# Low parts of the experts' first weights on VectorE in halves in place of GpSimd in quarters, and new places for all steps

## What is computed

```python
def _L0_xattn_ref(q, kv, mem, w_q, w_kv, w_concat):
    c = jnp.concatenate([mem, kv], axis=1)          # mem and kv are the same context
    qh = (q @ w_q).reshape(B, L, 16, 16).transpose(0, 2, 1, 3)
    k, v = split(c @ w_kv)
    attn_prob = softmax(einsum('bhid,bjd->bhij', qh, k) / sqrt(16))
    return (einsum('bhij,bjd->bhid', attn_prob, v)...) @ w_concat

def _L0_ffn_ref(x, ...):
    attn_out = layer_norm(residual, attn_nw, attn_nb)
    combine, dispatch = top1_gate(attn_out, wg, capacity)      # 8 experts, 256 rows each
    dispatched = einsum('sec,sm->ecm', dispatch, attn_out)
    h = gelu(einsum('ecm,emi->eci', dispatched, inter_w) + inter_b)      # 256 -> 1024
    expert_out = einsum('eci,eim->ecm', h, output_w) + output_b          # 1024 -> 256
    moe_out = einsum('sec,ecm->sm', combine, expert_out)
    rh = gelu(attn_out @ res_inter_w + res_inter_b)
    coef = softmax(attn_out @ res_coef)
    return (rh @ res_output_w + res_output_b) * coef[:, :1] + moe_out * coef[:, 1:] + residual

x = x + _L0_xattn_ref(_layernorm(x), ctx, ctx, ...)
x = x + _L0_ffn_ref(_layernorm(x), ...)
```

## Time and profile before

| | |
|---|---|
| median of 3 runs | 384.92 us (384.37 to 385.04) |
| the profiled execution | 384.03 us, span 382.3 us, mean granted clock 0.976 |
| TensorE matmuls | 339.3 us busy, 89% of the span |
| ScalarE | 222.4 us, 58% |
| VectorE | 217.9 us, 57% |
| GpSimd | 199.4 us, 52% |
| w1l on GpSimd | 50.7 us, 32 x 1.595 us |
| w2l on VectorE | 33.6 us, 32 x 1.073 us |
| hl on VectorE | 29.9 us, 32 x 0.945 us |
| DMA | 49.83 MB, mean 130 GB/s |

### The profile page before, as it was taken

The page is one execution under the profiler, slowest core; times in us unless marked ns, Lnnn a source line. Parts: engine busy times, 40 slices in busy tenths (PEclk is TensorE's granted clock), DMA queues, the critical chain, the costliest instruction groups (busy, mean ns, idle before and its releaser), DMA issues.

```text
span 382.3 us, 6412 instructions
## 1 busy us (share of the span) xinstructions
PE 339.3 (89%) x2234; PEld 276.1 (72%) x2234; DVE 217.9 (57%) x533; ACT 222.4 (58%) x429; POOL 199.4 (52%) x251
## 2 busy tenths in 40 slices
PE   3748889999999999999999999899989889889990
PEld 2535447767867867867866766788979889889990
DVE  4346547735625753763754632323589999798640
ACT  3312754863663563563663573629898698788630
POOL 4421421698374458358346424469366675677223
PEclk9966999999999999999999999999999999999997
DMA  6586596413144049046443001018443784795113
GB/s 182 182 238 181 165 294 234 124 56 96 44 123 123 0 138 313 5 146 163 146 135 98 2 16 41 3 56 271 114 154 64 226 259 111 235 260 143 16 15 41
DMA packets 51335, 49.83 MB, mean 130 GB/s; under 512 B 4764, under 2 KB 48488, under 8 KB 51304
## 3 DMA queue, kind: packets, MB, share of 16 engines
q1 hardware_dynamic: 48232, 45.21, 39.2%
q0 software_dynamic: 3072, 4.21, 5.6%
HBM read 33.65 MB, written 15.63 MB: 129 GB/s over the span
## 4 chain that ended last, share of the span: by engine, by line
PE 77%; DVE 6%; ACT 5%; issue 5%; DMA 3%; SPq 1%; POOL 1%; POOLq 0%; ACTq 0%
PE ubank L656 23%; PE mbank L838 15%; PE mbank L656 11%; PE pbank L741 4%; PE mbank L651 4%; PE sbank L709 4%; PE mbank L843 4%; PE mbank L844 3%; PE mbank L845 3%; PE sbank L731 3%; PE pbank L750 2%; DVE smax L1074 2%; ACT h L981 1%; DMA qstack<-dram_q 1%; DMA out_rows<-yrow,rowid 1%
## 5 line engine op out<-in xcount | busy, mean ns | idle before, releaser
L981 ACT ACTIVATE h<-ubank,vecT 128x256 f32<-128x256 f32 x128 | 53.1, 466 | 29.7 <-PE ubank L656 29.5
L838 PE MATMUL mbank<-w2r,h 128*128 128x256 f32 x256 | 62.0, 384 | 2.3 <-ACT h L981 1.0
L656 PE MATMUL ubank<-ao,w1r 128*128 128x256 f32 x256 | 59.7, 382 | 0.0
L612 POOL TENSOR_TENSOR w1l<-w1e,w1h 128x512 fp32r<-128x512 f32 x32 | 50.7, 1595 | 17.0 <-ACT w1h L859 16.8
L838 PEld LDWEIGHTS mbank<-w2r,h 128*128 128x128 f32 x256 | 46.9, 190 | 9.8 <-issue 2.6
L1074 DVE TENSOR_REDUCE smax<-sbank 128x4 f32<-128x512 f32 x64 | 42.0, 686 | 17.5 <-PE sbank L709 16.6
L656 PEld LDWEIGHTS ubank<-ao,w1r 128*128 128x128 f32 x256 | 47.0, 190 | 6.0
L915 ACT ACTIVATE p<-sbank 128x512 f32<-128x512 f32 x64 | 35.8, 596 | 17.4 <-PE sbank L731 17.4
L843 PE MATMUL mbank<-w2h,hh 128*128 128x256 f32 x128 | 36.9, 288 | 9.3 <-issue 7.4
L624 POOL DMA_INDIRECT out_rows<-yrow,rowid x16 | 26.6, 1663 | 29.7 <-DVE yrow L1213 28.5
L844 PE MATMUL mbank<-w2l,hh 128*128 128x256 f32 x128 | 36.0, 281 | 0.0
(11 more groups left out here) (139 smaller groups left out, 700.4 us busy)
## 6 DMA issues: line engine op xcount, KB each, us to landing
w1e<-in_L_ffn_inter_w SPq DMA_DIRECT2D x8, 1024.0 KB, 7.6
w2e<-in_L_ffn_output_w SPq DMA_DIRECT2D x8, 1024.0 KB, 11.0
qstack<-dram_q SPq DMA_DIRECT2D x16, 384.0 KB, 4.3
dram_q<-qpart SPq DMA_DIRECT2D x8, 384.0 KB, 2.7
dispatched<-zrow SPq DMA_DIRECT2D x4, 516.0 KB, 4.8
drow<-dispatched SPq DMA_DIRECT2D x8, 258.0 KB, 2.7
xs<-in_x SPq DMA_DIRECT2D x8, 256.0 KB
ctxs<-in_ctx SPq DMA_DIRECT2D x8, 256.0 KB
```

What stands on the lines that cost most here:

```text
L612: pool.tensor_tensor(quarter(w1l[e % SETS], q), w, quarter(w1h[e % 2], q).bitcast(f32), ALU.subtract).then_inc(sem("w1_low"), 1)
L656: last = nc.tensor.matmul(dst, w[kc], v[kc], start=(kc == 0), stop=(kc == len(w) - 1))
L838: last = nc.tensor.matmul(b[:, 0:D], h[:, n % 2, f, t * P:(t + 1) * P], w2[:, f, :], start=(f == 0), stop=(f == FC - 1))
L981: nc.scalar.activation(h[:, n % 2, f, :], place["up", n, c][:, j, :], ACT.Gelu_apprx_tanh, bias=vecT[:, col:col + 1]).then_inc(sem("gelu_d ...
```

## The change

- `Q` goes from 4 to 2: the copies of w1h and w2h on ScalarE and the low parts are done in halves of 128x1024 instead of quarters of 128x512.
- The low part of w1 (`ws1`) is no longer made by GpSimd, but by VectorE, with the same wait for w1_high and the same increment of w1_low.
- All tables of places and shifts have new numbers, so steps change their order on every engine.

In the expert stage the new order on TensorE is `down(e).0.0, .0.1, up(e+1).0, down(e).0.2, .0.3, up(e+1).1, up(e+1).2, ein(e+2), down(e).1.0, .1.1, up(e+1).3, down(e).1.2, .1.3`; before, `down(e).1.1` to `.1.3` stood behind `down(e+1).0.1`. On VectorE it is `ein(e+1), down(e-1).1, up(e).3, ws1(e+2).0, .1, down(e).0, ws2(e+1).0, up(e+1).0, ws2(e+1).1, up(e+1).1, up(e+1).2`. On ScalarE `ws1(e+2)` comes behind `up(e).3`, and `ws2(e+1)` behind `up(e+1).0`. On SyncE `w1load.3` goes ahead of `ein.3`, and `w1load.4` and `w2load.3` ahead of `ein.4`, and so on; the last `zero` goes from ahead of `gather.2.0` to behind `kspill.3`. In the units, among others, `vt` goes behind `B.3` and `loc` behind `B.4` on TensorE, `ctxT` of the next unit behind the first `up`, and `xT` behind the second `up`; on VectorE `gw` goes ahead of `loc`.

```diff
-    Q = 4
+    Q = 2
...
-    PERIOD = 32.05
-    OWN = [0.0, 14.14, 43.36, 72.72]
+    PERIOD = 31.98
+    OWN = [0.0, 13.94, 43.2, 72.27]
...
     EXPERT = {
-        "period": 14.26, "up": [-2.15, 0.91, 2.98, 4.31],
-        "down": [5.74, 6.08, 12.13, 12.6, 15.75, 20.68, 20.89, 24.81], "ein": [11.78], "first": [-3.16],
-        "ws1": [-24.43, -22.83, -20.42, -18.04], "ws2": [-4.21, -3.46, -0.71, -0.27], "w1load": [26.14],
-        "w2load": [48.57],
+        "period": 15.24, "up": [-3.77, -0.32, 1.13, 3.86],
+        "down": [5.66, 9.32, 11.73, 12.18, 16.23, 16.4, 19.42, 19.48], "ein": [12.14], "first": [-2.36],
+        "ws1": [-23.93, -23.41], "ws2": [-2.27, -1.67], "w1load": [31.31], "w2load": [47.77],
     }
...
-        def quarter(w, q):
-            return w[:, :, :].rearrange("p k f -> p (k f)")[:, 512 * q:512 * q + 512]
+        def part(w, q):
+            step = KC * F // Q
+            return w[:, :, :].rearrange("p k f -> p (k f)")[:, step * q:step * q + step]
...
-            def split(e, q):
-                pool.wait_ge(sem("w1_high"), Q * e + q + 1)
-                w = quarter(w1e[e % SETS], q)
-                pool.tensor_tensor(quarter(w1l[e % SETS], q), w, quarter(w1h[e % 2], q).bitcast(f32), ALU.subtract).then_inc(sem("w1_low"), 1)
...
-                copy(quarter(w1h[e % 2], q), quarter(w1e[e % SETS], q)).then_inc(sem("w1_high"), 1)
+                copy(part(w1h[e % 2], q), part(w1e[e % SETS], q)).then_inc(sem("w1_high"), 1)
...
-                copy(quarter(w2h[e % 2], q), quarter(w2e[e % SETS], q)).then_inc(sem("w2_high"), 1)
+                copy(part(w2h[e % 2], q), part(w2e[e % SETS], q)).then_inc(sem("w2_high"), 1)
...
+            def split1(e, q):
+                dve.wait_ge(sem("w1_high"), Q * e + q + 1)
+                V.tensor_tensor(part(w1l[e % SETS], q), part(w1e[e % SETS], q), part(w1h[e % 2], q).bitcast(f32),
+                                ALU.subtract).then_inc(sem("w1_low"), 1)
```

More of the change, by code:

```diff
@@ L95, in xattn_moe_ffn_kernel @@
     LAG_PE = {
-        "core": [0.73], "gate": [-1.05], "loc": [-0.42], "A": [-0.16], "B": [0.21], "PV": [-1.61], "part": [0.0],
-        "up": [-0.71], "down": [0.12], "oT": [1.46], "proj": [0.01], "M": [-0.32], "q": [0.75], "kv": [0.0],
-        "vt": [-1.05], "xT": [-2.24], "ctxT": [1.44], "ein": [-1.9], "vec": [-0.18],
+        "core": [0.73], "gate": [0.42], "loc": [-0.73], "A": [-0.31], "B": [0.15], "PV": [-2.25], "part": [-0.7],
+        "up": [-0.84], "down": [0.35], "oT": [1.52], "proj": [-0.17], "M": [-0.55], "q": [1.44], "kv": [0.6],
@@ L104, in xattn_moe_ffn_kernel @@
+        "ws1": [-1.12], "small": [3.84], "ws2": [-0.1],
     }
     LAG_DVE = {
[L106 to L108 removed]
+        "core": [-0.6], "gate": [0.07], "loc": [0.0], "A": [0.0], "gw": [-2.85], "o": [-0.98], "proj": [-0.12],
@@ L113, in xattn_moe_ffn_kernel @@
+        "bias": [-5.5], "down": [0.38], "qlast": [-0.2], "end": [-0.84], "small": [-0.06], "ws1": [1.57],
     }
     LAG_SP = {
-        "load": [-2.24], "kspill": [-6.58], "qspill": [0.0], "gather": [12.47], "M": [1.95], "wload": [-1.84],
-        "ein": [-4.43], "down": [0.29], "zero": [1.37], "late": [-1.25], "w1load": [5.67], "end": [1.61],
-        "small": [2.87], "w2load": [-1.34],
+        "load": [-4.81], "kspill": [-5.64], "qspill": [-0.35], "gather": [13.54], "M": [3.71], "wload": [0.2],
@@ L118, in xattn_moe_ffn_kernel @@
+        "ein": [1.22], "down": [7.99], "zero": [3.09], "late": [0.29], "w1load": [-0.02], "end": [-0.43],
+        "small": [0.55], "w2load": [0.66],
     }
     LOADS = {
-        "late": [-105.93], "vec": [25.54], "zero": [-7.35, -5.08, -1.48, 20.95],
-        "weights": [33.76, 49.58, 53.96, 66.7, 99.19],
+        "late": [-158.95], "vec": [21.72], "zero": [-0.17, 2.25, 6.33, 40.44],
+        "weights": [35.21, 40.56, 51.4, 69.68, 96.21],
     }
@@ L632, in _ @@
             calls = {"small": small, "ln1": ln1, "xn": norm_x, "kv": k_parts, "qlast": q_last, "ln2": ln2, "core": residual,
-                     "gw": scatter, "bias": bias, "ws1": split, "down": down, "end": end}
+                     "gw": scatter, "bias": bias, "down": down, "end": end}
             for step in order(LAG_POOL):
```

46 lines of the change are left out of this document (22 added, 24 removed), and 24 rows, old and new, of tables (AT, AT0, AT1).

## The result

The changed kernel takes 373.92 us in the median of four runs (371.57 to 374.39), the kernel before beside it 384.64 us. The ratio is 0.970 (0.966 to 0.974). A repeat of six runs gave 373.51 us and a ratio of 0.9663 (0.961 to 0.9716). So the change is worth 11 to 13 us. The forecast had 9.1 us less, 375.8 us.

The account below looks back on a forecast made before the run. TensorE, busy 89% of the span, was taken as the bound, with idle gaps in the experts. 384.03 - 10.0 (experts) + 0.6 (semaphores) + 0.3 (zero fill) = 374.9, plus 0.89 to the median: 375.8 us, range 373.2 to 381.0.

Parts of the forecast that it names:

- the start: Start of the kernel: reordered steps bounded by ±1.5 us, with 0.3 us added for the later last zero fill.
- the term of the units: Attention units: same matmul work in a full stage, so 0 us each, bounds -0.28 and +0.3 us.
- the experts' term: Experts: 10.0 us gained over six stretches, less 0.6 us that semaphores may still cost.
- GpSimd's arithmetic as the cause of the gap: Experts: GpSimd's w1l stretches VectorE's w2l by 2.1 us, so TensorE stands still for 1.70 us before down.
- on this the gain hangs: Experts: w1l leaving GpSimd ends the stretched VectorE operations, and the 10.0 us gain depends on that.
- these waits go, but add nothing: Experts: ScalarE's three waits for w1e, 3.8 us in all, vanish with earlier loads but add no further gain.
- the six stretches: Expert stages from 281.0 to 362.1 us: 81.10 us long, 9.29 us of it TensorE idle, 11.85 us content each.
- The 0.1 us per expert for semaphores: Experts: waits on semaphores that may remain after the change, 0.6 us in the sum.
- no new wait comes from the halves: Expert stage: the smallest reserve in the new order is 1.9 us, so nothing replaces the wait for w2_low.
- The second rival: Units and start also lose idle time and semaphores cost nothing: 372 to 374.5 us, chance 0.10.
- The zero fill: Start: last fill at about 73.5 us delays GpSimd's first scatter by 2 us; 0.3 us taken, at most 1.
- The rival of the scatters: Experts: GpSimd's scatters stretch VectorE's halves by 2.1 us each, 391 us; chance 0.07, including other large slowdowns.

Follow-up runs that it names:

- e2_new_order_pool: The kernel after, its new places and halves kept, with only w1l moved back to GpSimd, in halves; 379.41 us, ratio 0.9792.
- e1_old_order_dve: The kernel before, its places and quarters kept, with only w1l moved from GpSimd to VectorE; 385.27 us, ratio 0.9984.
- e8_dve_new_loads: e1_old_order_dve with SyncE's w1load and w2load put ahead of the row load in the experts; 374.43 us, ratio 0.970.
- e12_old_vt: The kernel after with only vt back in its old place on TensorE and VectorE, from unit 4 on; single execution 374.97 us.
- e13_old_loc: The kernel after with only loc back ahead of the fifth down step on TensorE, from unit 2 on; single execution 375.20 us.
- e7_zero_back: The kernel after with only the last zero fill moved 20 us earlier in SyncE's order, to its old place; 374.07 us, ratio 0.968.
- e3_new_quarters: The kernel after with Q = 4, quarters at the same places and w1l on VectorE; 373.25 us, ratio 0.9647.
- e5_old_experts: The kernel before, experts unchanged, with the steps of the attention units and the start in the order of after; 385.62 us, ratio 0.997.
- e10_pool_new_loads: The kernel before, w1l still on GpSimd, with only SyncE's w1load and w2load put ahead of the row load; 387.61 us, ratio 1.008.
- e17_finish_only: e1_old_order_dve with only TensorE ending an expert's down steps before it begins the next one's; 386.06 us, ratio 0.9985.

## Why the forecast fell short

*The sum.* Between the profiled executions of before and of the repeat lie 11.4 us (384.03 and 372.59); the sum had 9.1. The units give 2.1 us where it had 0, the experts 11.2 where it had 9.4 (10.0 less 0.6), and the start costs 2.0 where it had 0.3. So two steps failed: the term of the units, put at 0 with a bound of 0.28 us each, and the size of the experts' term. That the error is not larger is luck of the start, whose cost hides part of both.

*GpSimd's arithmetic as the cause of the gap.* As a wait that ends last it was read rightly, and `e2_new_order_pool` shows that it still holds back 4.3 us in the new order. What failed is "on this the gain hangs": `e1_old_order_dve` removes GpSimd's part and gains nothing, `e8_dve_new_loads` adds the loads' place and gains 11 us. In "these waits go, but add nothing" the accounting holds, since the 10.0 us take in all of the idle time in the six stretches; as a cause the loads were taken for a bystander, while their place, or VectorE's and TensorE's together, is what lets the gain come at all. The prediction didn't ask what w1l in VectorE's queue does to yrow and, through SyncE, to the next load. That the forecast came near is owed to the new order, which opens that ring in two ways.

*The size in the experts.* The six stretches of 81.10 us were to become 6 x 11.95 us; they are 6 x 11.79 us. The 0.1 us per expert for semaphores isn't there, and the content is 11.79, not 11.85 us: 1.0 us. Another 0.8 to 0.9 us was outside the six stretches, where the sum left the times as they were. TensorE's idle time from ein of expert 0 to ein of expert 1 fell from 0.74 to 0.23 us, and the short idle times ahead of 281 us went as well.

*VectorE and ScalarE.* A half costs 1.218 and 1.222 us, against 1.21. VectorE is busy for 9.45 us per stage (10.2 expected), ScalarE for 10.9 (at most 11.2). "More operations" was wrong, the count is the same. That no new wait comes from the halves is right, and the comparison with quarters shows that halves weren't needed.

*The attention units* were put at 0, with -0.28 us as the best. The full ones are 0.35 us shorter each, beyond that bound, since matmuls also follow each other faster. From the first proj to ein of expert 0 it is 2.1 us, of which 0.5 us lies ahead of the third proj. This is the largest term that was missed in the sum. What shortens the matmuls' distances is known as far as `e12_old_vt` and `e13_old_loc` go: the places of vt and loc. The second rival ("more than the experts", 372 to 374.5 us, a chance of 0.10) had the outcome, by the units and the semaphores, though not by the start.

*The start* was put at +0.3 us with ±1.5. The zero fill was issued at 76.00 us, later than the 73.5 worked out, the first scatter starts at 81.32, and VectorE waits longer than foreseen, as these rows of GpSimd, VectorE and TensorE in the kernel after show (answering):

```profile
80.12 3.69 PE L833 MATMUL mbank<-w2r,h 128*128 128x256 f32 x16 [0.45 <-DVE gd L1130]
...
81.32 1.25 POOL L596 DMA_INDIRECT dispatched<-core,slot  x1 [0.65 <-POOL core L590]
...
85.78 0.48 DVE L1203 SCALAR_TENSOR_TENSOR xs<-mbank,coef,xs 128x256 f32<-128x256 f32 x1 [4.71 <-POOL xs L606]
```

It costs nothing all the same, by `e7_zero_back`. The rest of the start's new order costs about 1 us, within the bound; that it is the A and B steps was not tried. The clock was not in the sum at all.

*The rival of the scatters* (391 us) did not come. Where the two meet it is the scatter that gives way, as the last section shows, and nobody waits for it. The hl of 3.07 us at 282.22, on which the rival rests, had GpSimd's w1l beside it as well; in `e1_old_order_dve`, without that, an hl begun within a scatter (284.83) takes 0.68 us.

## What to carry to other kernels

Taking away the last-ending wait is worth only the distance to the next limit, and moving an operation into another in-order queue makes a limit of its own: follow what stands behind it there through every queue back to the operation's own input. If that path closes, add it up as a ring and hold it against the stage. Here 13.78 us stood against 11.8, and it could be opened at the load, or by reading a finished bank ahead of the work that needs the load, with TensorE finishing that bank early enough.

## What the runs showed of the hardware

A scatter of GpSimd takes 1.54 us alone, 1.83 us in the median beside quarters on VectorE (`e1_old_order_dve`, `e3_new_quarters`) and 2.16 us beside halves. Two stretches of the timeline of the kernel after:

```profile
293.56 1.22 DVE L1182 TENSOR_TENSOR w2l<-w2e,w2h 128x1024 fp32r<-128x1024 f32 x1 [0.33 <-ACT w2h L854]
294.02 2.20 POOL L619 DMA_INDIRECT out_rows<-yrow,rowid  x1 [2.60 <-DVE yrow L1213]
...
294.70 0.68 DVE L1191 TENSOR_TENSOR hl<-h,hh 128x512 fp32r<-128x512 f32 x1
...
295.30 1.22 DVE L1182 TENSOR_TENSOR w2l<-w2e,w2h 128x1024 fp32r<-128x1024 f32 x1
...
301.28 2.35 DVE L1177 TENSOR_TENSOR w1l<-w1e,w1h 128x1024 fp32r<-128x1024 f32 x2
301.55 2.36 POOL L619 DMA_INDIRECT out_rows<-yrow,rowid  x1 [5.33 <-DVE yrow L1213]
```

The subtraction keeps its 1.22 us, and the scatter, begun second, pays up to 0.8 us. The subtractions begun while the scatter is under way (294.70, 295.30) keep their times too: a scatter does not hold VectorE up here. GpSimd's arithmetic does: in `e2_new_order_pool` a yrow begun behind its w1l paid 4.0 us. The Trainium skill ("SBUF — State Buffer", section "Who interferes with whom") has it that whoever issues first gets the shared pair for its whole instruction. That the later one waits agrees with this; the length doesn't, since the first half of GpSimd ended at 307.65 and yrow waited on until the second, begun at 307.01 behind it, was through. Nor do the starts in the trace decide it each time: before, the second of the two w2l that the earlier trace rows shows as one row began at 297.41 and took 2.78 us although GpSimd's w1l began only at 297.79. The page infers that a subtraction of two SBUF inputs leaves the descriptor work of such a scatter alone; here the scatter is longer, and the measurement decides. Which part of the scatter waits isn't shown.

A long wait of TensorE can cost more than itself. In four profiles (`e1_old_order_dve`, `e5_old_experts`, `e10_pool_new_loads`, `e17_finish_only`) the granted clock fell to 1.2 GHz once within the experts, for 3.4 us, with TensorE busy again. It had stood still for 2.39, 2.21, 1.67 and again 0.70, and 2.40 us shortly before. Single waits of 1.64 and 1.68 us in the kernel before were followed by no fall. In the fall, matmuls follow each other every 0.213 us in place of 0.119, and the stage has 1.5 us more of TensorE work, as shown above.

The same load of 1024 KB takes 7.5 to 8.9 us when it is issued together with the row load and that of w2 (`e1_old_order_dve`), and 4.9 to 5.5 us when the three are spread (`e8_dve_new_loads`): the ring's longest piece depends on what shares its start.
